# Picking the first operation from raw x, and turning later weights from fourfold copies

## What is computed

```python
x = x + conv_attention(_ln_c(x))            # block 1
t = _to_tokens(x)
t = t + _L0_ffn_ref(_ln_t(t), ...)          # block 2: scan over 33 steps
x = x + deformable_conv(_ln_c(x))           # block 3: L1_conv_w_off, L1_conv_w
t = t + expert_ffn(_ln_t(t))                # block 4: L1_ffn_gate_w

def step(h, p):                             # of block 2
    op = jnp.argmax(h[0, 0, :NOPS])         # 19 operations, chosen by the first pixel
    ...                                     # attention with the op's weights
    h = jnp.where(p['am'][op], y, h)
    z = jax.nn.relu(h @ p['w1'][op] + p['b1'][op]) @ p['w2'][op] + p['b2'][op]
    h = jnp.where(p['fm'][op], z, h)
```

## Time and profile before

| | |
|---|---|
| median of 3 runs | 129.36 us (129.30 to 129.49) |
| span of the profiled execution | 127.3 us (the page gives no other time for it) |
| median less span | 2.06 us |
| TensorE busy | 114.2 us, 90% of the span |
| VectorE busy | 74.4 us, 58% |
| ScalarE busy | 68.3 us, 54% |
| GpSimd busy | 25.9 us, 20% |
| chain of waits, by engine | PE 59%, DVE 21%, ACT 12% |

### The profile page before, as it was taken

One profiled execution on the slowest core, in us unless ns is written; L12 is line 12 of the kernel. 1 busy time (PEld: TensorE's weight loads), 2 busy tenths in 40 slices (PEclk: granted clock), 3 DMA queues, 4 the chain that ended last, 5 costly groups with the idle time before them and its releaser, 6 DMA issues.

```text
span 127.3 us, 3032 instructions
## 1 busy us (share of the span) xinstructions
PE 114.2 (90%) x1200; PEld 82.3 (65%) x1201; DVE 74.4 (58%) x149; ACT 68.3 (54%) x121; POOL 25.9 (20%) x34
## 2 busy tenths in 40 slices
PE   6989889998989899997977899999999987989990
PEld 5667566577423325877966678888888975656750
DVE  0076976718984362129999599699493004346241
ACT  4254796357630407027978959969956631347000
POOL 8996000004940000002616050050000000000000
PEclk9999999999999999999999999999999999999997
DMA  3544000000101000000000000000000000000002
GB/s 106 168 56 110 12 0 5 0 1 8 34 0 31 3 17 14 5 5 0 0 0 5 0 0 5 0 0 5 0 8 0 0 8 0 0 0 0 5 0 88
DMA packets 3060, 2.22 MB, mean 17 GB/s; under 512 B 1570, under 2 KB 2754, under 8 KB 3040
## 3 DMA queue, kind: packets, MB, share of 16 engines
q0 software_dynamic: 464, 0.67, 2.7%
q1 hardware_dynamic: 2144, 0.74, 2.4%
q10 hardware_dynamic: 432, 0.55, 1.2%
HBM read 1.68 MB, written 0.26 MB: 15 GB/s over the span
## 4 chain that ended last, share of the span: by engine, by line
PE 59%; DVE 21%; ACT 12%; issue 6%; DVEq 0%; ACTq 0%
PE ps L977 9%; PE ps L489 5%; DVE smat L913 5%; PE ps L991 5%; PE ps L1001 4%; PE ps L1293 4%; PE ps L514 3%; PE ps L496 3%; PE ps L276 3%; PE ps L287 3%; ACT tx L848 2%; DVE smatT L740 2%; PE ps L518 2%; PE ps L655 2%; ACT rstd L530 2%
## 5 line engine op out<-in xcount | busy, mean ns | idle before, releaser
L913 DVE TENSOR_TENSOR smat<-ty,tx 128x1536 f32<-128x1536 f32 (+1 forms) x14 | 21.5, 1555 | 4.3 <-ACT tx L848 4.2
L954 ACT ACTIVATE smatT<-ps 128x1536 f32<-128x1536 f32 x12 | 17.4, 1450 | 7.8 <-PE ps L977 7.6
L977 PE MATMUL ps<-cst,smat 128*128 128x128 f32 x144 | 18.1, 275 | 2.6 <-DVE smat L913 2.3
L977 PEld LDWEIGHTS ps<-cst,smat 128*128 128x128 f32 x144 | 15.7, 140 | 4.3 <-DVE smat L913 3.2
L489 PE MATMUL ps<-cst 128*128 128x256 f32 x48 | 13.0, 387 | 0.3 <-issue 0.3
L1001 PE MATMUL ps<-samp,wc 128*128 128x128 f32 x72 | 11.0, 291 | 0.0
L991 PE MATMUL ps<-smatT,xt 128*32 128x96 f32 x384 | 10.4, 249 | 0.4 <-ACT samp L945 0.4
L1001 PEld LDWEIGHTS ps<-samp,wc 128*128 128x128 f32 x72 | 8.9, 191 | 1.6
L489 PEld LDWEIGHTS ps<-cst 128*128 128x128 f32 x48 | 8.3, 190 | 2.2 <-issue 1.3
L830 POOL TENSOR_SCALAR disty<-disty 128x288 f32<-128x288 f32 x3 | 6.2, 2081 | 17.2 <-ACT disty L837 17.2
L991 PEld LDWEIGHTS ps<-smatT,xt 128*32 128x32 f32 x384 | 7.9, 109 | 2.3 <-issue 1.8
(11 more groups left out here) (200 smaller groups left out, 198.1 us busy)
## 6 DMA issues: line engine op xcount, KB each, us to landing
cst<-in_cst ACTq DMA_DIRECT2D x1, 278.0 KB, 3.5
x<-in_x SPq DMA_DIRECT2D x2, 128.0 KB, 2.9
ew<-in_L_ffn_weight POOLq DMA_DIRECT2D x4, 64.0 KB, 2.2
ew<-in_L_ffn_weight POOLq DMA_DIRECT2D x1, 256.0 KB, 4.2
w<-in_L_ffn_ffn_w SPq DMA_DIRECT2D x3, 64.0 KB
cst<-in_cst ACTq DMA_DIRECT2D x1, 129.0 KB, 3.0
out<-fin SPq DMA_DIRECT2D x1, 128.0 KB, 2.2
out<-fin ACTq DMA_DIRECT2D x1, 128.0 KB, 2.1
```

The lines of the kernel that those rows point to most:

```text
L913: return nc.vector.tensor_tensor(smat[:, n % 3, BP * part.start:BP * part.stop, :].rearrange("p u (g r c) -> p (u g) r c", g=DG, c=W), ty[ ...
L954: nc.scalar.activation(smatT[:, n % 2, :, :, :].rearrange("p k g n -> p (k g n)"), ps[:, bank:bank + 3, :].rearrange("p b n -> p (b n)"), ...
L977: last = nc.tensor.transpose(ps[:, bank + u // BP, (u % BP) * P:(u % BP + 1) * P], smat[:, n % 3, u, :], ident)
```

## The change

The first pick is made from x itself. TensorE reads column 0 of x as soon as the first half of x is written, ahead of the norm's centring, and VectorE picks before it writes any of u. u is then written in two whole halves. The two `keep_clock` after the norm and the fifteen `keep_warm` are gone.

The three weights of the later blocks are loaded four times side by side, so that each transpose gives 128 partitions. ScalarE copies w_off out of PSUM once, VectorE copies w and gate_w once together into a new tile wst, and GpSimd multiplies wst with a 0/1 mask (ownc) into wc and gwt, which makes zeroing wc unnecessary. ebcol is made by GpSimd at the start. The wait for wc and gwt (c_we) stands on TensorE before the deformable part; the wait for c_wd before block 3's first matmuls is gone.

```diff
...
@@ -163,11 +162,12 @@
         b2 = sb("b2", [P, 2])
         rcol = sb("rcol", [HID, 1])
 
-        woff_n = sb("woff_n", [OCH, C * TAPS])
-        wc_n = sb("wc_n", [C, C * TAPS])
+        woff_n = sb("woff_n", [OCH, BP, C * TAPS])
+        wc_n = sb("wc_n", [C, BP, C * TAPS])
         woff = sb("woff", [P, TAPS, OPAD])
         omc = sb("omc", [P, BP, N])
         wc = sb("wc", [P, TAPS, BP, C])
+        wst = sb("wst", [P, TAPS * C + E])
         ccol = sb("ccol", [P, 3])
         boff = sb("boff", [P, OCH])
         offb = sb("offb", [P, OCH])
@@ -199,7 +199,7 @@
         bn = sb("bn", [P, 9])
         ebcol = sb("ebcol", [E, E * B])
 
-        gw_n = sb("gw_n", [E, C])
+        gw_n = sb("gw_n", [E, BP, C])
         gwt = sb("gwt", [P, J, E, BP, J])
         gb = sb("gb", [P, 1])
         ew1 = sb("ew1", [P, E // BP, HID])
@@ -633,7 +633,7 @@
                 pass
 
             def cleared(self, pe):
-                pe.wait_ge(sem("c_wa"), 2 * BP)
+                pe.wait_ge(sem("c_wa"), 1)
                 pe.wait_ge(sem("c_wd"), 1)
                 pe.wait_ge(sem("clear_pe"), 1)
 
@@ -1157,13 +1157,16 @@
         @block.gpsimd
         def _(pool):
             nc.gpsimd.memset(a4t[:, :, :], 0.0).then_inc(sem("zero_a4"), 1)
-            nc.gpsimd.memset(wc[:, :, :, :], 0.0).then_inc(sem("zero_c"), 1)
             nc.gpsimd.memset(r4[:, :, :], 0.0).then_inc(sem("zero_r4"), 1)
             nc.gpsimd.memset(woff[:, :, :], 0.0).then_inc(sem("zero_c"), 1)
             nc.gpsimd.memset(gwt[:, :, :, :, :], 0.0).then_inc(sem("zero_c"), 1)
-            pool.dma_start(woff_n[:, :], dr("L1_conv_w_off").rearrange("o c a b -> o (c a b)")).then_inc(sem("ld_c"), 16)
-            pool.dma_start(wc_n[:, :], dr("L1_conv_w").rearrange("o c a b -> o (c a b)")).then_inc(sem("ld_c"), 16)
-            pool.dma_start(gw_n[:, :], dr("L1_ffn_gate_w")).then_inc(sem("ld_c"), 16)
+
+            def beside(ap):
+                return ap.unsqueeze(1).broadcast_to([ap.shape[0], BP, ap.shape[1]])
+
+            pool.dma_start(woff_n[:, :, :], beside(dr("L1_conv_w_off").rearrange("o c a b -> o (c a b)"))).then_inc(sem("ld_c"), 16)
+            pool.dma_start(wc_n[:, :, :], beside(dr("L1_conv_w").rearrange("o c a b -> o (c a b)"))).then_inc(sem("ld_c"), 16)
+            pool.dma_start(gw_n[:, :, :], beside(dr("L1_ffn_gate_w"))).then_inc(sem("ld_c"), 16)
             pool.dma_start(boff[:, :], dr("L1_conv_b_off").partition_broadcast(P)).then_inc(sem("ld_c"), 16)
             pool.dma_start(ccol[:, :], every_pair(dr("L1_conv_col"))).then_inc(sem("ld_d"), 16)
             pool.dma_start(gb[:, :], dr("L1_ffn_gate_b").rearrange("(e k) -> e k", k=1).unsqueeze(1).broadcast_to(
@@ -1175,7 +1178,10 @@
             w2_ = dr("L1_ffn_weight2").rearrange("e h o -> h e o")
             pool.dma_start(ew2[:, :, :], w2_[0:HID, :, :]).then_inc(sem("ld_d"), 16)
             pool.dma_start(eb2[:, :], dr("L1_ffn_weight2")[:, HID, :]).then_inc(sem("ld_d"), 16)
-            pool.wait_ge(sem("b_u"), 3)
+            pool.wait_ge(sem("ld_cst"), 16)
+            nc.gpsimd.tensor_copy(ebcol[:, :].rearrange("p (e b) -> p e b", b=B),
+                                  ident[0:E, 0:E].unsqueeze(2).broadcast_to([E, E, B])).then_inc(sem("c_eb"), 1)
+            pool.wait_ge(sem("b_u"), J)
             summed(nc.gpsimd)
             nc.gpsimd.memset(xwin[:, :, 0:XTOP, :], 0.0).then_inc(sem("zero_x"), 1)
             nc.gpsimd.memset(xwin[:, :, XTOP + H:, :], 0.0).then_inc(sem("zero_x"), 1)
@@ -1183,6 +1189,17 @@
             for g in range(DG):
                 other = slice(CG * (1 - g), CG * (1 - g) + CG)
                 nc.gpsimd.memset(xtw[:, :, g, :, :, other], 0.0).then_inc(sem("zero_x"), 1)
+            pool.wait_ge(sem("c_wd"), 1)
+            pool.wait_ge(sem("zero_c"), 2)
+            shape = [P, TAPS, BP, C]
+            nc.gpsimd.tensor_tensor(wc[:, :, :, :],
+                                    wst[:, 0:TAPS * C].rearrange("p (t o) -> p t o", o=C).unsqueeze(2).broadcast_to(shape),
+                                    const("ownc").unsqueeze(1).unsqueeze(3).broadcast_to(shape),
+                                    ALU.mult).then_inc(sem("c_we"), 1)
+            for j in range(J):
+                nc.gpsimd.tensor_tensor(gwt[:, j, :, :, j], wst[:, TAPS * C:].unsqueeze(2).broadcast_to([P, E, BP]),
+                                        const("ownc").unsqueeze(1).broadcast_to([P, E, BP]),
+                                        ALU.mult).then_inc(sem("c_we"), 1)
             tents_pool(pool)
 
         @block.scalar
@@ -1198,12 +1215,8 @@
             norm_act(act, 2, eps5)
             act.wait_ge(sem("c_w"), 1)
             act.wait_ge(sem("zero_c"), 2)
-            for g in range(BP):
-                rows = slice(C * g, C * g + C)
-                nc.scalar.activation(woff[rows, :, 0:OCH], ps[0:C, 2, 0:TAPS * OCH].rearrange("c (t o) -> c t o", o=OCH),
-                                     ACT.Copy).then_inc(sem("c_wa"), 1)
-                nc.scalar.activation(wc[rows, :, g, :], ps[0:C, 3, 0:TAPS * C].rearrange("c (t o) -> c t o", o=C),
-                                     ACT.Copy).then_inc(sem("c_wa"), 1)
+            nc.scalar.activation(woff[:, :, 0:OCH], ps[:, 2, 0:TAPS * OCH].rearrange("c (t o) -> c t o", o=OCH),
+                                 ACT.Copy).then_inc(sem("c_wa"), 1)
             act.wait_ge(sem("table"), 16)
             recurrent(act, ACTBody())
             norm_act(act, 3, eps6)
@@ -1260,28 +1273,31 @@
 
             def weights_of_3():
 
+                woff_taps = woff_n[:, :, :].rearrange("o g (c t) -> o (g c) t", t=TAPS)
+                wc_taps = wc_n[:, :, :].rearrange("o g (c t) -> o (g c) t", t=TAPS)
                 pe.wait_ge(sem("ld_c"), 64)
                 for tap in range(TAPS):
-                    nc.tensor.transpose(ps[0:C, 2, tap * OCH:(tap + 1) * OCH].rearrange("c (t k g) -> c t g k", t=3, g=DG),
-                                        woff_n[:, tap::TAPS], ident[0:OCH, 0:OCH])
+                    last = nc.tensor.transpose(
+                        ps[:, 2, tap * OCH:(tap + 1) * OCH].rearrange("c (t k g) -> c t g k", t=3, g=DG),
+                        woff_taps[:, :, tap], ident[0:OCH, 0:OCH])
+                last.then_inc(sem("c_w"), 1)
                 for tap in range(TAPS):
-                    nc.tensor.transpose(ps[0:C, 3, tap * C:(tap + 1) * C], wc_n[:, tap::TAPS], ident[0:C, 0:C])
-                nc.tensor.transpose(ps[0:C, 4, 0:E], gw_n[:, :], ident[0:E, 0:E]).then_inc(sem("c_w"), 1)
+                    nc.tensor.transpose(ps[:, 3, tap * C:(tap + 1) * C], wc_taps[:, :, tap], ident[0:C, 0:C])
+                nc.tensor.transpose(ps[:, 3, TAPS * C:TAPS * C + E], gw_n[:, :, :].rearrange("e g c -> e (g c)"),
+                                    ident[0:E, 0:E]).then_inc(sem("c_w"), 1)
 
             att_pe(pe, "a_", [a4t[:, n, :] for n in range(4)], "a_u", keep_clock)
-            norm_pe(pe, 2, lambda j: (sem("a_x"), j + 1), 2)
-            pe.wait_ge(sem("b_u"), 1)
-            nc.tensor.matmul(ps[0:1, 5, 0:C], u[0:C, 0:1], ident[0:C, 0:C], start=True, stop=True).then_inc(sem("b_col"), 1)
+            pe.wait_ge(sem("a_x"), 1)
+            nc.tensor.matmul(ps[0:1, 5, 0:C], x[0:C, 0:1], ident[0:C, 0:C], start=True, stop=True).then_inc(sem("b_col"), 1)
+            norm_pe(pe, 2, lambda j: (sem("a_x"), j + 1), 0)
             weights_of_3()
-            pe.wait_ge(sem("b_u"), 3)
+            pe.wait_ge(sem("b_u"), J)
             pe.wait_ge(sem("table"), 16)
-            keep_warm(15, 7)
             keep_long(2, 7)
             recurrent(pe, PEBody())
             norm_pe(pe, 3, lambda j: (sem("l_xs"), j + 1), 0, src=xs)
             keep_long(2, 5)
 
-            pe.wait_ge(sem("c_wd"), 1)
             pe.wait_ge(sem("c_u"), J)
             for tap in (CENTER, *range(CENTER), *range(CENTER + 1, TAPS)):
                 ki, kj = tap // K, tap % K
@@ -1344,7 +1360,7 @@
                     last = nc.tensor.transpose(ps[:, 1, i * P:(i + 1) * P], u[:, i * P:(i + 1) * P], ident)
                 last.then_inc(sem("e_ut"), 1)
                 pe.wait_ge(sem("ld_d"), 16 * 9)
-                pe.wait_ge(sem("c_wd"), 2)
+                pe.wait_ge(sem("c_eb"), 1)
                 nc.tensor.matmul(ps[:, 6, 0:E * B], eb1[:, :], ebcol[:, :], start=True, stop=False)
                 nc.tensor.matmul(ps[:, 7, 0:BP * C].rearrange("p (g o) -> p g o", g=BP), ebcol[:, :],
                                  eb2[:, :].unsqueeze(1).broadcast_to([E, BP, C]), start=True, stop=False)
@@ -1393,6 +1409,7 @@
                 wide_pe(pe)
                 to_end()
 
+            pe.wait_ge(sem("c_we"), 1 + J)
             by_fit(pe, fit_to_end, wide_to_end)
 
         @block.vector
@@ -1426,21 +1443,13 @@
                 dve.wait_ge(sem("a_wo"), j + 1)
                 nc.vector.scalar_tensor_tensor(out=x[:, half], in0=ps[:, j, 0:N], scalar=acol[:, 3:4], in1=x[:, half],
```

(19 more changed lines are left out.)

## The result

| | before | after |
|---|---|---|
| median | 129.33 us (129.21 to 129.49) | 135.74 us (134.84 to 137.08) |
| span of the profiled execution | 127.3 us | 133.0 us |
| granted clock, mean over the span | 0.995 | 0.962 |

The account below looks back on a forecast made before the run. The bound was the wait chain from attention's end to the first FFN matmul (L652), with TensorE's sequencer last after the change. 1.13 us gained less 0.1 at the start gave 1.03: 129.36 to 128.3 us, range 127.3 to 129.1.

Parts of the forecast that it names:

- The loads of w1: Ahead of L652: the earlier pick lets SyncE load w1 2.9 us earlier, there at 31.3, no longer last.
- u, its price for the pick's matmul: In the norm: the pick's matmul ahead of the centring costs 0.22 us; u is whole at 30.22 instead of 30.44.
- the sequencer's 2.85 us: TensorE's walk from L570 to L652, started at 30.27, comes last: L652 at 33.12, stage 1.13 us shorter.
- the choice: Ahead of the loop: TensorE's sequencer can't enter early while keepers wait for u, so its 2.85 us start at 30.27.
- The weight turns: Nineteen wider transposes behind the norm: 2.6 us at most, hidden under the sequencer's time; cost nothing, at most 0.1.
- The start: Program start: larger, earlier GpSimd loads delay the attention weights, 0 to 0.68 us on the path; taken as 0.1.
- the sum of bytes over the DMA engines' free share: Program start: extra load bytes at 390 GB/s, engines busy 0.48, give 0 to 0.94 us delay, 0.26 covered.
- Rival 2: Program start: bigger loads hold up attention by the full 0.68 us; gain 0.45, time 128.9 us; chance 0.12.
- Rival 3: Before L652: new copies' wait or slower fetch of loop code keeps the stage at 34.25; 129.3 to 129.5 us; chance 0.06.
- rival 4: From 28 to 33 us: fewer keepers let the granted clock fall, costing 2.2 to 4.4; about 131 us; chance 0.07.
- The pause before L977: Evidence against rival 4: a TensorE pause of 0.78 us there passes without a fall of the clock.
- L514's 1.92 us: Evidence for rival 4's price: four passes take 1.92 us at the start, 1.03 later, read as the lower clock level.

Follow-up runs that it names:

- e4: Changed kernel with GpSimd's loads held until the attention weights landed and TensorE's code put back in its old place by small matmuls: 128.91 us, ratio 0.998.
- e10: e4 without TensorE's wait for u ahead of the loop, one long keeper instead of two, two keepers and 19 small matmuls at the start: 128.40 us, ratio 0.994.
- e3: Changed kernel with 17 matmuls more at the start of TensorE's program, so later code stands where it stood before: 133.13 us.
- e9: e4 with the two 256-column keepers put back ahead of the weight turns and two one-element matmuls taken out: 130.38 us.
- e1: Changed kernel with GpSimd's loads issued only when the attention weights have landed: 131.70 us.
- e2: Kernel before with the three loads fourfold, still issued behind the memset of wc: 130.00 us, ratio 1.005.
- e7: Kernel before with fourfold loads as in e2, and the memset of wc moved behind them: 133.78 us, ratio 1.038.
- e6: e5 without its nine narrow keepers and nine small matmuls, so 17 matmuls fewer ahead of the loop than in the kernel before: 132.44 us.
- e5: Kernel before with only the pick from x and whole halves of u, narrow keepers and small matmuls keeping the code's place: 129.47 us, ratio 1.001.
- e12: e5 with ebcol made by GpSimd, TensorE's wait for u and the narrow keepers removed, code's place kept: 129.07 us, ratio 0.999.
- d1: As e3 but with two keepers and 10 small matmuls, 8 matmuls fewer ahead of the loop than in the kernel before: 137.84 us, one run.
- d2: As e3 but with one keeper and 36 small matmuls, 17 more ahead of the loop than in the kernel before: 136.72 us, one run.

## Why the prediction was wrong

- **The loads of w1: right.** The pick starts at 30.89, 1.99 us behind L362 (before: 4.89), and SyncE issues the load 3.90 behind it (before: 6.81): 2.9 us earlier in the stage, both; no DMA releases L652 in the changed kernel.
- **u, its price for the pick's matmul, and the sequencer's 2.85 us: right.** The pick's matmul takes 0.21; e4 shows entry at u and about 2.85 us from there. e10 shows what the choice hung on: without the wait the sequencer does go in ahead of u, and then the turns and one keeper decide.
- **The weight turns: right while the clock holds.** 2.38 us from 33.02 to 35.40, under the 2.6 at most. In e4 they are hidden as priced: the keepers behind them end at 33.39, before the sequencer is through. In e3 and e9 those keepers end last, because they take 3.5 and 3.65 us at the half clock.
- **The start: the term that was mis-sized.** Put at 0.1, at most 0.68; it was 3.3 of waiting plus the clock behind it, 4.6 in the trace and 4.0 in the time (e1). The step that failed is the sum of bytes over the DMA engines' free share. It treats small and large loads as if they were served at once and evenly, and takes the lead of 1 us for harmless; e2 and e7 show 0.8 and 2.5. The packets of the changed kernel show what the sum missed: from 5.5 to 9.5 us SyncE's queue gets only 171 small packets through (4.3% of the engines' time) among 299 of GpSimd's (65.7%), although 30% of that time is free; in e1, with none of GpSimd's there, SyncE's are through by 6.3. Rival 2 had the mechanism with the wrong bound.
- **The sequencer's walk: a cost left out.** 2.85 us were carried over as a constant. 0.49 of them were a branch that depends on where the code stands, and the change takes 17 matmuls out of that code: 2.9 us in the trace, 2.6 in the time from the changed kernel to e3 and 2.8 from e1 to e4. The trace of before already had the price of a long branch, 3.48 us at L798, which the prediction doesn't use. Rival 3 names "a slower fetch of the loop's code", but as something that gives back a gain, not as a price of its own.
- **The clock: rival 4's fall came, its price not.** The clock falls at three places; the first, at the start, rival 4 doesn't have. At the keepers it is hidden under the branch, and the third, in the first FFN step, costs nothing that shows: from L652 to that of the second step are 7.32 us, as before (7.31). In e10's trace the first step does cost 1.45 us more, and in e4 about 0.7 us lie between the means of the runs with a lower mean clock and the others. The pause before L977 was a poor witness against it. Nor are L514's 1.92 us a row at the lower level: the granted clock reads 1.00 there. The rows that show its price are L496 here (3.62 instead of 1.91) and L655 in e10.

The conv over the offset weights takes 3.98 us after and 4.46 before; that is most of the 0.7 us won behind L652. e6, with the old copies, has 3.98 too, so the single copy isn't the cause; it stays open.

## What to carry to other kernels

A load that isn't needed for 20 us can cost most at the start: give the small loads that something waits for a lead, or hold the large ones back by a semaphore. After deleting instructions ahead of a loop or a branch, look at the branch's own duration in the new profile before explaining anything else; a few tiny matmuls put the code back. Two late things that end together (the sequencer and eight copies) have to be shortened together, as e5, e12 and e10 show between them.

## What the runs showed of the hardware

- TensorE's branch over the attention body takes 0.34 to 0.73 us or 3.2 to 3.8, by its place in the code: 8 and 17 matmuls fewer ahead of it give the long one (d1, e6), the old place and 17 more the short one (e3, d2).
- Small loads of one queue end later beside large ones of another: 16 KB of bvrow held VectorE until 9.50 us beside 243 and 144 KB, until 5.99 without (e1).
- The granted clock fell to 0.50 behind the nineteen wide weight turns, with TensorE counted as busy for 5.36 of the 5.40 us before (e9); two long keepers then took 3.65 us instead of 1.98 (e4).
